# Block products for gate and up from FFN block 1 on, in a two-layer transformer kernel

## The reference

```python
x = x + attn(layernorm(x))            # x @ W_qkv + b, softmax(q k^T / sqrt(32), causal) v, @ W_out + b
x = x + ffn(layernorm(x))             # (silu(x @ Wg^T) * (x @ Wu^T)) @ Wd^T
```

## Time and profile before

| | |
|---|---|
| median of 3 runs | 1985.8 us |
| the profiled execution | 1981.08 us |
| its span | 1979.4 us |
| PE busy | 1954.9 us, 10288 matmuls |
| POOL busy | 982.2 us |
| DVE busy | 1159.8 us |
| ACT busy | 805.8 us |

### The profile page before, as it was taken

How to read it: one execution, slowest core, us unless ns; L and a number is a source line. 1 busy time by engine, 2 the same in 40 slices (tenths; PEclk the granted TensorE clock), 3 DMA queues, 4 the chain that set the end, 5 groups by cost and what they waited for, 6 DMA issues and landing times.

```text
span 1979.4 us, 27849 instructions
## 1 busy us (share of the span) xinstructions
PE 1954.9 (99%) x10288; PEld 1442.3 (73%) x10288; DVE 1159.8 (59%) x2387; ACT 805.8 (41%) x1478; POOL 982.2 (50%) x767
## 2 busy tenths in 40 slices
PE   7999999999999999999999999999999999999999
PEld 6655588888866568888885656888888565688887
DVE  5777455445677745544567774445457777544544
ACT  2487522221258752222116774322221686432221
POOL 5314469763230436976433053797534215289740
PEclk9999999999999999999999999999999999999999
DMA  5333111121333311311253331121113333012111
GB/s 161 95 88 76 34 43 54 54 64 43 85 87 76 76 44 32 107 53 54 75 139 87 76 76 44 36 62 53 53 43 86 87 80 82 24 43 64 54 43 43
DMA packets 58821, 132.37 MB, mean 67 GB/s; under 512 B 10560, under 2 KB 11584, under 8 KB 58688
## 3 DMA queue, kind: packets, MB, share of 16 engines
q1 hardware_dynamic: 58688, 130.60, 24.2%
HBM read 75.51 MB, written 4.19 MB: 40 GB/s over the span
## 4 chain that ended last, share of the span: by engine, by line
PE 94%; ACT 2%; DVE 2%; DMA 1%; SPq 1%; issue 1%; POOL 0%; ACTq 0%; DVEq 0%; POOLq 0%
PE bank L1354 11%; PE bank L1356 11%; PE bank L1355 11%; PE bank L1488 11%; PE ring L1354 11%; PE ring L1355 11%; PE ring L1356 11%; PE bank L1461 8%; PE ring L1430 7%; PE ring L1345 1%; ACT prob L861 1%; SPq L555 1%; DMA area<-kq_parts 1%; ACT kq_parts L844 0%; ACT area L940 0%
## 5 line engine op out<-in xcount | busy, mean ns | idle before, releaser
L861 ACT ACTIVATE prob<-bank 128x512 f32<-128x512 f32 (+1 forms) x512 | 273.1, 570 | 158.5 <-PE bank L1461 133.0
L655 POOL TENSOR_SCALAR area<-w_stage 128x1024 fp32r<-128x1024 f32 x126 | 144.3, 1146 | 374.2 <-PE bank L1356 190.0
L657 POOL TENSOR_TENSOR area<-w_stage,area 128x1024 fp32r<-128x1024 f32 x126 | 302.0, 2397 | 10.5
L1168 DVE TENSOR_TENSOR x<-x,bank 128x512 f32<-128x512 f32 x256 | 170.4, 684 | 232.2 <-PE bank L1356 231.6
L732 POOL TENSOR_SCALAR_AFFINE_SELECT prob<-prob 128x512 f32<-128x512 f32 x128 | 82.7, 647 | 446.5 <-ACT prob L861 356.1
L1098 DVE CUSTOM_DVE_ANT_0 xn<-ring,mask_row 128x384 bf16<-128x384 f32 (+7 forms) x384 | 244.2, 663 | 66.8 <-PE ring L1430 65.3
L1354 PE MATMUL ring<-xt_hi,area 128*128 128x512 f32 x672 | 263.7, 392 | 1.3 <-DVE area L1201 1.3
L1355 PE MATMUL ring<-xt_lo,area 128*128 128x512 f32 x672 | 262.0, 390 | 0.0
L1356 PE MATMUL ring<-xt_hi,area 128*128 128x512 f32 x672 | 261.8, 390 | 0.0
L1461 PE MATMUL bank<-area 98*128 98x512 f32 (+3 forms) x768 | 244.7, 374 | 2.6 <-ACT prob L861 1.4
L1461 PEld LDWEIGHTS bank<-area 98*128 98x128 f32 x768 | 133.1, 188 | 125.1 <-ACT prob L861 83.6
(11 more groups left out here) (172 smaller groups left out, 3612.5 us busy)
## 6 DMA issues: line engine op xcount, KB each, us to landing
w_stage<-ffn_w SPq DMA_DIRECT2D x96, 512.0 KB, 3.5
area<-kq_parts SPq DMA_DIRECT2D x336, 128.0 KB, 2.4
w_stage<-attn_w SPq DMA_DIRECT2D x32, 512.0 KB, 4.3
area<-attn SPq DMA_DIRECT2D x48, 128.0 KB, 4.0
x<-x_in SPq DMA_DIRECT2D x16, 256.0 KB, 3.9
out<-x SPq DMA_DIRECT2D x16, 256.0 KB, 2.0
bias_rows<-row_bias SPq DMA_DIRECT2D x8, 256.0 KB, 3.9
masked<-x_in SPq DMA_DIRECT2D x4, 256.0 KB, 4.2
```

The source lines that it names most:

```text
L655: pool.tensor_scalar(hi, src, 1.0, 0.0, ALU.mult, ALU.add).then_inc(w_hi_done, 1)
L657: pool.tensor_tensor(lo, src, hi.bitcast(F32), ALU.subtract).then_inc(w_split, 1)
L861: act.activation(prob[:, step % PROB_BUFS, h, off:], scores_at(u, j, h), ACT.Exp, scale=SCALE).then_inc(prob_ready, 1)
L1168: dve.tensor_tensor(x[:, t, :], x[:, t, :], row_bank(s, n)[:, :], ALU.add).then_inc(rows_drained, 1)
```

## The change

1. `QUAD_FIRST` becomes 1, so that block 1 is made by the seven products too. The steps 2 and 3 are no longer made by `gate_up`, and the block products begin right after step 1.
2. Slots 11 and 12 (gate and up of block 1) now need sums. They are split out of `POOL_ORDER`, the last one after the last d; before, they were split in the loop behind it, once the second chunk was normalised. SP's loads up to slot 13 are in `SP_ORDER`.
3. The high parts of slots 13 and 14 are made by ACT (`weights_to_hi`), behind the hidden tile of step 1; POOL makes their low parts.
4. ACT and DVE split the four token sums during step 1 instead of steps 1 to 3.
5. The first x tiles have a semaphore each. At the start statistics, reciprocal deviation and normalisation go by pairs of tiles, DVE makes the low parts of the V weights, and a memset of POOL (L767 before) stands behind the first split.
6. The five tables of letters are written anew. Each has as many of each letter as before, but for w (8, now 10) in `POOL_ORDER` and l (9, now 11) in `SP_ORDER`.

```diff
-QUAD_FIRST, QUAD_LAST = 2, BLOCKS - 2
+QUAD_FIRST, QUAD_LAST = 1, BLOCKS - 2
...
-DIFF_STEPS = (2, 3)
 DIFFS_AT = FFN_SLOT0 + 5
+CAST_BY_ACT = (FFN_SLOT0 + 5, FFN_SLOT0 + 6)
+SPLITS_BEFORE, LOADS_BEFORE = FFN_SLOT0 + 5, FFN_SLOT0 + 6
...
-    "bbdwbwwmmmbbmwbmbmmmmmmmmmmmmmmmawaawammammmmwmmabamdmmmwd",
+    "dwmmbmwbbbmmmwmmmmmwbmwmmmmmmmmbaawammabmmmmammbaawdmmmmwwdw",
...
-    "lkkklkklkkkmkkkmkllkkmkkkkkkmklkkkmkkkkmkkkmklmll",
+    "kkkkkklkklmkkmlkkkkklkmlkkkkmkkmkkkkklkmkkkmlklmlll",
...
-        x_loaded = [sem(f"x_loaded{c}") for c in range(CHUNKS)]
+        x_loaded = [sem(f"x_loaded{t}") for t in range(TT)]
...
-                    loads = iter(range(AHEAD, FFN_SLOT0 + 4))
+                    loads = iter(range(AHEAD, LOADS_BEFORE))
...
+                if j in CAST_BY_ACT:
+                    low_part(it, n, j)
+                    return
...
+                hi, src = w_part(j, slice(0, SLOT))[0], w_stage[:, j % 2, :]
+                pool.tensor_scalar(hi, src, 1.0, 0.0, ALU.mult, ALU.add).then_inc(w_hi_done, 1)
+                low_part(it, n, j)
+
+            def low_part(it, n, j):
+
-                pool.tensor_scalar(hi, src, 1.0, 0.0, ALU.mult, ALU.add).then_inc(w_hi_done, 1)
                 pool.wait_ge(w_hi_done, n + 1)
                 pool.tensor_tensor(lo, src, hi.bitcast(F32), ALU.subtract).then_inc(w_split, 1)
...
+            for r in range(2):
+                pool.wait_ge(var_ready, r + 1)
+                t = slice(2 * r, 2 * r + 2)
+                pool.tensor_tensor(rstd[:, t], var_eps[:, t], minus_half[:, 0:2], ALU.pow).then_inc(rstd_ready, 1)
+            pool.wait_ge(rstd_ready, 2)
+            pool.wait_ge(w_split, len(V_SLOTS))
+            for i in range(len(V_SLOTS), AHEAD):
+                split_weights(0, i)
+            pool.wait_ge(w_split, AHEAD)
             pool.memset(k_stack[3 * HEAD:3 * HEAD + 2, 1:, :, :].bitcast(F32), 1.0).then_inc(ones_ready, 1)
             pool.wait_ge(ones_ready, 1)
-            inverse_deviation(0, 0, 0)
-            pool.wait_ge(xn_ready, CT)
-            for i in V_SLOTS:
-                hi, lo = w_part(i, slice(0, SLOT))
-                pool.wait_ge(w_hi_done, i + 1)
-                pool.tensor_tensor(lo, w_stage[:, i, :], hi.bitcast(F32), ALU.subtract).then_inc(w_split, 1)
-            for i in range(len(V_SLOTS), AHEAD):
-                split_weights(0, i)
...
-                splits = iter((AHEAD, *range(QK_SLOT0 + 2, FFN_SLOT0 + 3)))
+                splits = iter((AHEAD, *range(QK_SLOT0 + 2, SPLITS_BEFORE)))
...
-                for i in range(FFN_SLOT0 + 3, SLOTS + (2 if it < LAST else 0)):
+                for i in range(SPLITS_BEFORE, SLOTS + (2 if it < LAST else 0)):
...
+                def weights_to_hi(j):
+
+                    act.wait_ge(w_split, it * SLOTS + CAST_BY_ACT[0])
+                    act.wait_ge(w_loaded[j % 2], (it * (SLOTS // 2) + j // 2 + 1) * 16)
+                    act.wait_ge(ring_full, full(it, ("gu", 1, BT - 1)))
+                    act.activation(w_part(j, slice(0, SLOT))[0], w_stage[:, j % 2, :], ACT.Copy).then_inc(w_hi_done, 1)
...
-                for s in range(1, QUAD_STEPS[0]):
-                    for t in range(BT):
-                        silus(s, t)
-                        hidden_hi(s, t)
-                        if s in (1, 2):
-                            diff_to_hi((s - 1) * BT + t)
+                silus(1, 0)
+                hidden_hi(1, 0)
+                diff_to_hi(0)
+                diff_to_hi(1)
+                diff_to_hi(2)
+                silus(1, 1)
+                hidden_hi(1, 1)
+                for j in CAST_BY_ACT:
+                    weights_to_hi(j)
+                diff_to_hi(3)
...
+            def first_normalise(r):
+
+                dve.wait_ge(rstd_ready, r + 1)
+                for t in (2 * r, 2 * r + 1):
+                    dve.tensor_scalar(xn_tile(t), x[:, t, :], mean_var[:, t, 0:1], rstd[:, t:t + 1],
+                                      ALU.subtract, ALU.mult).then_inc(xn_ready, 1)
+
+            def first_weights_lo(i):
+
+                hi, lo = w_part(i, slice(0, SLOT))
+                dve.wait_ge(w_hi_done, i + 1)
+                dve.tensor_tensor(lo, w_stage[:, i, :], hi.bitcast(F32), ALU.subtract).then_inc(w_split, 1)
...
-                for s in range(1, QUAD_STEPS[0]):
-                    for t in range(BT):
-                        hidden_parts(s, t)
-                        if s in DIFF_STEPS:
-                            diff_to_lo(BT * DIFF_STEPS.index(s) + t)
-                    for d in downs_after(s):
-                        add_rows(d)
+                hidden_parts(1, 0)
+                diff_to_lo(0)
+                hidden_product(1, 1)
+                diff_to_lo(1)
+                hidden_lo(1, 1)
+                diff_to_lo(2)
+                diff_to_lo(3)
...
-            chunk_stats(0, 0)
-            normalise_pair(0, 0, 0)
-            normalise_pair(0, 0, 1)
+            for t in range(CT):
+                dve.wait_ge(x_loaded[t], 16)
+                tile_stats(t, x[:, t, :])
+                if t % 2:
+                    variances(t + 1, range(t - 1, t + 1))
+            first_normalise(0)
+            first_weights_lo(0)
+            first_normalise(1)
             xt_to_lo(0, 0, 0)
+            first_weights_lo(1)
             xt_to_lo(0, 0, 1)
```

More of the change, by code:

```diff
@@ L212 @@
+    "sfsfssfssfssfssfsvfsssfvsffvfvvffspffpff",
+    "sspfssfvffsspsffsvsfsvsffsvfssvsfsfsvfssfvvsfsfsvsfsvffssssvfssfssvvf",
+    "ssfvvfssffffsfsvsfsfvsfsppssssvffpfsfsvffp",
+    "sfsfvfsfvfsfsffsfsfsfsfsfsfsfvsfsvffssvffssvsfsfssfsfsfssssfvssfssf",
+    "svvsfffsvfsspsspsssvvvvffsssspfsfsv",
+    "sfsvsffspsffsvsffsfsfsvsfsffsfsfsvfsfssfsfsvsfsfsvsssffssssvssf",
+    "sfsfssfvvssffvssffsssvvfsssvssf",
+    "ssvvssfssvssvssvvssffssfssfssvssvvvssfssfssssvvvssssvvv",
 )
 ACT_ORDER = (
-    "xxxxxxx",
@@ L464, in s_sums, with deviations @@
             return lo.rearrange("p (i n) -> p i n", n=2 * P)
+        def deviations(it, ln, c):
+            return it * 2 * CHUNKS + ln * CHUNKS + c + 2
         def rows_taken(it, row):
@@ L597, in _ @@
                         load_biases(1 - layer)
-                    for i in range(FFN_SLOT0 + 4, SLOTS + (AHEAD if it < LAST else 0)):
+                    for i in range(LOADS_BEFORE, SLOTS + (AHEAD if it < LAST else 0)):
                         if i == STAGE_BEFORE and it < LAST and first_layer(it + 1):
@@ L740, in add_out_bias @@
                     if first_layer(it):
-                        pool.wait_ge(x_loaded[t // CT], (it // LAYERS + 1) * (16 * CT))
+                        for n in range(t, t + CT):
+                            pool.wait_ge(x_loaded[n], (it // LAYERS + 1) * 16)
                     pool.wait_ge(xn_ready, it * 2 * TT + t + CT)
@@ L1017, in chunk_variance, with variances @@
                 n = it * 2 * TT + ln * TT + (c + 1) * CT
-                dve.wait_ge(stats_done, 2 * n - CT)
-                for t in range(c * CT, (c + 1) * CT):
+                variances(n, range(c * CT, (c + 1) * CT))
+            def variances(n, tiles):
+                dve.wait_ge(stats_done, 2 * n - len(tiles))
+                for t in tiles:
                     dve.bn_aggr(mean_var[:, t, :], stats[:, t, :]).then_inc(stats_done, 1)
                 dve.wait_ge(stats_done, 2 * n)
-                t = slice(c * CT, (c + 1) * CT)
+                t = slice(tiles[0], tiles[-1] + 1)
                 dve.tensor_scalar(var_eps[:, t], mean_var[:, t, 1], EPS, None, ALU.add).then_inc(var_ready, 1)
+            def first_normalise(r):
[7 more added lines that the diff above has]
+                dve.tensor_tensor(lo, w_stage[:, i, :], hi.bitcast(F32), ALU.subtract).then_inc(w_split, 1)
             def late_stats(it, t):
-                if t == CT and it == 0:
-                    dve.wait_ge(x_loaded[1], 16 * CT)
+                if it == 0:
+                    dve.wait_ge(x_loaded[t], 16)
                 elif t == CT and first_layer(it):
```

49 lines of the change are left out of this document (20 added, 29 removed).

## The result

The changed kernel takes **1992.8 us** (median of 8 runs, 1990.6 to 1995.8) where the kernel before took 1986.2 beside it (8 runs, 1981.7 to 1988.0): ratio 1.0038, 95% interval 1.0029 to 1.0048. It is slower by 0.4%, some 7 us ("same" in the forecast meant under 0.2% apart). The forecast was 1987.9 with a range of 1974 to 1996.

The account below looks back on a forecast made before the run. PE, busy for 99% of the span, was taken as the bound, with POOL lacking slack before block 2. Terms -10.9 + 16 - 3.0 + 0 = +2.1 us on the median 1985.8 gave 1987.9 us, range 1974 to 1996.

Parts of the forecast that it names:

- the second rival: Second normalisation on DVE collides with POOL's slot 12 sums; +4.8 us, so +6.9 in all, 1992.7 us; chance 0.25.
- Term 1, matmuls: Block 1 by seven products: 12 fewer matmuls per iteration, 48 in four, at 0.2267 us each: -10.9 us.
- 10240: Sign in the trace after: 10240 matmuls in place of 10288.
- Term 2, the wait for slot 15: At m1 (up) of block 2 PE waits for POOL's split of slot 15, about 4 us per iteration: +16 us.
- The gap at m1: Sign in PE's timeline: about 4 us before block 2's seventh matmul, released by POOL's slot 15; forecast wrong if under 2.
- Term 3, the start: Start by pairs of tiles: full matmuls from about 13.3 us instead of 16.67; -3.0 us, between 0 and -3.4.
- The fourth rival: The start does not gain, since POOL's 5.2 us memset and its next deviation come later: +5.1, 1990.9 us; chance 0.05.
- Term 4, the tables: New tables of attention hold the same instructions, so 0 us, between -5 and +5.
- An attention half over 1 us longer: Sign that the forecast is wrong: the attention half over 1 us shorter or longer.
- The iterations' first silus: Sign, FFN to FFN: iterations about 490.8 us apart against 489.3 to 489.6 before.

Follow-up runs that it names:

- e11: Changed kernel with old tables, early memset, slot 15's high part by ACT, its low part first, slot 12 after the normalised rows: 1971.1 us, 0.9937 of before.
- e12: Kernel before with only the new start and POOL's memset ahead of the first deviations: 1979.3 us, ratio 0.9980 to before.
- e5: Changed kernel with ACT writing low parts of token sums 2 and 3 as plain copies, DVE's subtractions left out: 1986.9 us, ratio 1.0011 to before.
- e2: Changed kernel with POOL's memset moved ahead of the first deviations in the first iteration: 1991.5 us, ratio 1.0037 to before.
- e1: Changed kernel with attention's five letter tables of before, plus two w and two l added at the ends: 1994.4 us, ratio 1.0053 to before.
- e6: Changed kernel with attention's tables of before, early memset, and slot 15's high part also cast by ACT: 1983.6 us, ratio 0.9992 to before.
- e3: Changed kernel with block 1 made directly again and no casts by ACT, new start and tables kept: 1987.6 us, ratio 1.0022 to before.
- e7: Changed kernel with its new tables, early memset, and slot 15's high part also cast by ACT: 1983.2 us, ratio 0.9987 to before.
- e10: Changed kernel with new tables, early memset, slot 15's high part by ACT, its low part first, slot 12 after the normalised rows: 1974.6 us, 0.9951 of before.
- e8: Changed kernel with block 1 made directly again, no casts by ACT, and the early memset: 1989.2 us, ratio 1.0014 to before.

## Why the prediction was right, and where it was not

The range held; the point, +2.1, was 4.5 us short of the medians' 6.6 and 8.1 short of the profiled pair's 10.2. By the forecast's own line of 0.2% the kernel is slower and not the same: the whole interval, 0.29 to 0.48%, lies above it. That the median is almost the 1992.7 of the second rival is chance, since that mechanism cost PE nothing here. Of the 8.1 us the FFN has 0.3 (forecast +5.1, measured +5.4), the start 2.6 (forecast -3.0, measured -0.4 at the 71st matmul) and attention 5.3 (forecast 0; +2.1 in iteration 0, +3.2 in the other three). By its terms:

- **Term 1, matmuls: right.** 10240, and e11 against e12 gives its worth where the wait is small: 6.8 us less in four FFN stretches, which is nearly 10.9 and four times the 0.24 us that PE had waited at block 2 of before, less four waits of 1.2 at m6 (7.1).
- **Term 2, the wait for slot 15: right.** The forecast had POOL's chain at 39.8 us and PE's loss at 3.8 to 4.0 us; measured 39.6, and 1.3 + 2.4 = 3.7. The gap at m1 alone is 2.4 and not the 4 that was to be seen there, because 1.3 was already lost at m6. m1 starts when POOL's chain ends, so m6's lateness is part of the 3.7 and not on top, as forecast. The two 1.0 us holds that e5 could remove were shown to be DVE's; the other two stayed in e5, where their DVE instructions stayed. The rule of the Trainium skill (SBUF — State Buffer, Who interferes with whom) is that a DVE instruction with two SBUF inputs contends with a GpSimd instruction that reads SBUF: e5's 2.37 against 3.37 agrees.
- **Term 3, the start: failed.** -3.0 was taken; 0.4 was left behind the start. The fourth rival, with a chance of 0.05, named POOL's memset and the size, though not this way of holding PE. e2 shows 3.3 us for the memset, and e12 that the start alone is worth 4.0. What the forecast missed is that a DVE instruction of 0.17 us can be held up to the end of a 5.2 us MEMSET (20.47 to 24.93), with the PSUM drain behind it in DVE's queue. The MEMSET and this instruction did not meet in the trace of before, but the hold could be read there: the same instruction took 0.65 to 1.00 us in each of the four iterations when it stood beside POOL's addition of biases, and ended some 0.03 us behind it. So the remark at the second rival that no row shows `tensor_scalar` and POOL together is wrong. The forecast also left out that the clock rises earlier with the new start, worth 1.0 us in the changed kernel and 2.1 in e12. Iteration 1 of before:

```profile
514.47 2.55 POOL L743 TENSOR_TENSOR x<-x,bias_rows 128x512 f32<-128x512 f32 x2
516.04 1.00 DVE L1023 TENSOR_SCALAR var_eps<-mean_var 128x4 f32<-128x4 f32 x1
```

- **Term 4, the tables: failed in size.** 0 was taken, within 5; attention was 5.3 us longer, 3.4 of it at low clock. An attention half over 1 us longer was also one of the forecast's own signs that it is wrong: the three took 1.07 more each. From the 71st matmul of 512 columns to the first silu the old tables take 225.1 to 225.8 us (before, e1, e6, e11, e12). The new ones take 226.0 in e3, e7 and e10, whose clock does not fall there, and 227.1 to 228.6 in the other six, whose clock does; so much of what they cost there comes through the clock. The earlier start is not the cause, since e12 has it, and behind 20 us no start of PE there comes over 1 us after the one before. With everything else equal, e11 has 3.5 us less than e10 (by medians; the ratios 0.9937 and 0.9951 have overlapping intervals), of which 1.5 lie before the first silu. In e10 PE waits 1.6 to 2.5 us (start to start) for kq_parts in every iteration, in e11 nowhere. As the view of waits names it, the new order brings PE to a score tile before the transfer of kq_parts that it needs. Counting pairs of score tiles said nothing of that; the due time of each transfer would have.
- **Missing: the clock.** Three stretches of 3.41 us at 1.2 GHz, 1.7 us each, **5 us in all**, two in attention (88.12 and 1562.68) and one in the FFN (which is why it takes 1.5 us more in iteration 0). Without it the FFN would have come out 1.4 us under the forecast. A wait of PE was priced at its length and 0.2 for the restart. Between the medians the clock counts for less, since the kernel before has such stretches too in most executions: its mean granted clock is mostly 0.998, that of the changed kernel 0.997, an estimated 2 us of the 6.6.

The iterations' first silus lay 491.6 to 492.8 us apart, where 490.8 was forecast. Of the rivals, the second was real as a mechanism and free in the changed kernel by a hair: PE did not wait there, and did in e1, e3, e6 and e8 by 0.9 to 1.1 us. The Trainium skill (SBUF — State Buffer, Who interferes with whom) says of a DVE instruction in a 2-port mode, which `tensor_scalar` can enter, that whoever issues first gets the pair for the whole instruction and the other "fully blocks"; e3's 3.73 and the 4.46 beside the memset agree.

What stays open: m6's wait of 1.2 to 1.3 us was left in every version with the seven products in block 1. That ACT's copy of m1 behind the cast of the fourth sum sets it is argued from the named releaser and from e5, and was not tried by another order on ACT.

## What to carry to other kernels

Price a helper's work by its place in its queue, not by its busy share: the whole gain of 48 matmuls hung on which of POOL's pieces for one slot came first, and putting the one that PE reads first in front, with a semaphore of its own, was worth 5.6 us, where the products alone had been worth 1.4. When a change puts waits of the lengths seen here (from 1.7 us) in front of a busy TensorE, add the chance that its clock falls behind them. And when an early step is pulled forward, look at what long instruction of the neighbour engine it now stands beside.
